# All first keys ahead of the query projection, the projection in three fp32r products, and the input's norm on ScalarE

## The chip, the cores and the metric

The kernel runs on one core of a Trainium2 chip. The metric is the time of one execution on the device in microseconds (us). The engines of the core are TensorE (PE: products and transposes; its weight loads are listed apart as PEld), VectorE (DVE), ScalarE (ACT), GpSimd (POOL) and SyncE (SP, which here only issues loads and stores). They work side by side and wait for each other by semaphores. On each engine the instructions run in the order in which they stand in the program.

## What is computed

A layer of three parts, in fp32, on 8 batches of 64 tokens (512 rows of 512 numbers):

```python
x = x + xattn(layernorm(x), ctx, mask, q_w, q_b, k_w, k_b, v_w, v_b)
x = x + attn(layernorm(x), W_q)
x = x + ffn(layernorm(x), gate_w, gate_b, w1, b1, w2, b2)

def xattn(h, context, mask, ...):          # 16 heads of 32, 1601 context rows per batch
    q = split_heads(h @ q_w.T + q_b)
    k = split_heads(context @ k_w.T + k_b)
    v = split_heads(context @ v_w.T + v_b)
    scores = einsum('bhqd,bhkd->bhqk', q, k) / sqrt(32)
    probs = softmax(where(mask, -inf, scores))
    return join_heads(einsum('bhqk,bhkd->bhqd', probs, v))
```

`attn` is a self-attention without softmax, `ffn` a mixture of 8 experts of which each row takes 2. The change is about the start of `xattn`: the first layernorm, the query projection and the keys of the first batch.

## The kernel before

**Split numbers.** A full fp32 product of 512 columns takes 0.86 us in the profile (the 16 of the query projection take 13.75 us). Most products are made instead from two parts of each operand: the high part is the number rounded to fp32r, the low part the difference to it. `PASSES` lists three products, high by high, high by low, low by high, and `products()` (L847 in its loop) makes them one behind the other for each of the four pieces of 128 rows (C = 4). ACT makes a high part by copying (`copy`, L586, into `kw[0]`, `vw[0]`, `cx[0]`), DVE or POOL the low part by subtracting (`weight_lo` L1287, `ctx_lo` L525, into `cx[1]`). `plain()` (L854) multiplies unsplit fp32 numbers in one product; the query projection uses it, on `qwraw` and the turned input `xnT`.

**Chunks and keys.** The context of a batch arrives in four chunks of 416 columns (`load_chunk`, into the two halves of `raw`). A key item is one of 8 for half of the heads: chunk k = j // 2, row block m = j % 2. PE multiplies into one of four banks (`work`), ACT writes the high part with the bias (`key_hi`, L599), DVE the low part (`key_lo`, L1310), and that frees the bank (`w_free`). In the first batch the loads of chunk 0 and of the first half of the key weights are cut in two by rows (`FIRST_C`, `REST_C`), so that work can start on the first half of the rows. Chunks 0 and 1 get their low parts from DVE, chunks 2 and 3 from POOL.

**The start, on each engine.** SP issues: key weights and chunk 0 in halves, chunk 1, x (`xin`), the query weights (`qwraw`), chunks 2 and 3 (each waits for the low part of the chunk whose half of `raw` it takes), value weights, the other half of the key weights, mask, a second copy of x (`xs`) and the value bias. All go through one hardware queue. PE: keys 0 and 1 (L941, key 0 whole and then key 1), keys 2 and 3, 16 transposes of the normalised input (L950), keys 4 and 5, the query projection (four tiles of 512 tokens into the banks `yb`, that is ptp0 to ptp2 and pv), keys 6 and 7, and then the first batch's body. DVE takes the statistics of `xin` (L1256), and after ACT's root (`root`, L594) a few steps of 4 columns (L1268 to L1272); it then scales the four tiles of `xin` (L1276), which raises `ln1`. ACT copies the transposed tiles to `xnT`, and the projection with the bias to `qT` (L650). DVE builds the blocks `qbd` from `qT` (`query_blocks`, L1324 and L1328), the left operand of the score products (L885). PE may begin them when the blocks, the low parts of all weights (`w_lo`) and an empty bank are there.

**The body** of a batch runs over two halves of the heads. `STEPS` lists its pieces in order: score pairs, value items (two groups of 128 context rows, L847 into `ptp`), exponentials, transposes of the probabilities (L976), weighted sums (L992), and the next keys. POOL's `ctx_lo` for the next batch runs in the second half of each body. POOL also adds the value bias to `xs` (L533, four tiles), which is read after the last batch; this stands between the chunks of batch 0 and those of batch 1.

## Time and profile before

| | us |
|---|---|
| median of 3 runs | 1274.7 |
| lowest and highest of them | 1272.16 and 1274.91 |
| the profiled execution | 1274.62 |
| its span, first to last instruction | 1272.9 |

| part of the program | us from the start of the span |
|---|---|
| PE's first product of keys | 6.4 |
| transposes of the normalised input | 20.5 |
| query projection | 28.7 |
| first score products | 46.9 |
| first value product | 49.1 |

The profile is of one execution. Its page gives busy times per engine and groups of instructions. The timeline lists instructions in order of time, and in brackets how long the engine had been idle before one and what ended that (the releaser). Equal instructions in a row are merged (x4). Matmuls overlap, so the duration of one is longer than the distance from start to start; what a row of them costs is read from the starts. The granted clock of TensorE is a share of 2.4 GHz.

### The profile page before, as it was taken

To read this page: it belongs to the slowest core of one execution; us is meant where nothing else is said; L and a number is where in the kernel's file an instruction comes from. 1 tells how busy PE (TensorE), PEld (TensorE's weight loads), DVE (VectorE), ACT (ScalarE), POOL (GpSimd) and SP (SyncE) were. 2 spreads that over 40 slices of the span, in tenths; PEclk is the share of its full clock that TensorE was granted. 3 is DMA by queue.
4 is the path that set the end of the run, shared out by engine and by line. 5 is a ranking of instruction groups with operands and counts; after the bars stand their busy time and mean duration, and the time that the engine had idled before them with its cause. 6 is when DMAs were issued, how large, how long until landed. Compare 5 with 4: busy or idle time off the path is not lost.

```text
span 1272.9 us, 22193 instructions
## 1 busy us (share of the span) xinstructions
PE 1237.2 (97%) x8493; PEld 1154.6 (91%) x8493; DVE 843.7 (66%) x2197; ACT 674.5 (53%) x1195; POOL 159.3 (13%) x87
## 2 busy tenths in 40 slices
PE   6999999999999999999999999999989999999997
PEld 5799999999999999999999999989768889889896
DVE  4565666566665666656566665686768887877876
ACT  5344544645544553554555446434544767676672
POOL 2203100400310130040022004000022000000011
PEclk9999999999999999999999999999979999999999
DMA  9002200220220031022004002200327677776763
GB/s 333 28 1 88 84 1 1 92 81 1 92 80 1 5 124 44 1 92 80 1 28 144 1 1 92 97 1 1 110 75 259 233 244 263 229 249 235 247 218 103
DMA packets 61683, 129.23 MB, mean 102 GB/s; under 512 B 3660, under 2 KB 21208, under 8 KB 61336
## 3 DMA queue, kind: packets, MB, share of 16 engines
q1 hardware_dynamic: 59416, 121.03, 27.4%
q0 software_dynamic: 2176, 6.95, 1.7%
q8 instruction: 61, 1.00, 0.3%
q14 instruction: 30, 0.25, 0.1%
HBM read 122.07 MB, written 15.34 MB: 108 GB/s over the span
## 4 chain that ended last, share of the span: by engine, by line
PE 91%; DVE 5%; ACT 2%; DMA 1%; issue 1%; POOL 0%; SPq 0%; DVEq 0%; POOLq 0%
PE ptp L847 24%; PE work L847 20%; PE work L1146 8%; PE pv L992 7%; PE ptp L976 7%; PE work L885 6%; PE work L1148 4%; PE ptp L1165 2%; PE ptp L1166 2%; PE ptp L1168 2%; PE ptp L1167 2%; PE ptp L1169 2%; PE work L854 1%; DMA raw<-in_ctxT 1%; DVE pt L1401 1%; ACT pt L586 1%
## 5 line engine op out<-in xcount | busy, mean ns | idle before, releaser
L847 PE MATMUL ptp<-vw_hi,cx_hi 128*128 128x256 f32 x832 | 241.8, 291 | 0.0
L847 PE MATMUL ptp<-vw_hi,cx_lo 128*128 128x256 f32 x832 | 235.4, 283 | 0.0
L847 PE MATMUL ptp<-vw_lo,cx_hi 128*128 128x256 f32 x832 | 235.4, 283 | 0.0
L525 POOL TENSOR_TENSOR cx_lo<-raw,cx_hi 128x1664 fp32r<-128x1664 f32 x30 | 113.8, 3792 | 667.0 <-ACT cx_hi L586 667.0
L847 PE MATMUL work<-cx_hi,kw_hi 128*128 128x400 f32 (+1 forms) x504 | 175.1, 347 | 3.0 <-POOL cx_lo L525 1.7
L847 PEld LDWEIGHTS ptp<-vw_hi,cx_hi 128*128 128x128 f32 x832 | 159.3, 192 | 17.0 <-issue 17.0
L847 PE MATMUL work<-cx_hi,kw_lo 128*128 128x400 f32 (+1 forms) x504 | 173.8, 345 | 0.0
L847 PE MATMUL work<-cx_lo,kw_hi 128*128 128x400 f32 (+1 forms) x504 | 173.4, 344 | 0.0
L1401 DVE TENSOR_TENSOR pt<-ptp,pt 128x512 fp32r<-128x512 f32 (+1 forms) x224 | 141.1, 649 | 34.0 <-ACT pt L586 30.4
L1310 DVE SCALAR_TENSOR_TENSOR kk_lo<-work,biasT,kk_hi 128x400 fp32r<-128x400 f32 (+1 forms) x128 | 78.9, 632 | 122.4 <-ACT kk_hi L599 121.8
L847 PEld LDWEIGHTS ptp<-vw_lo,cx_hi 128*128 128x128 f32 x832 | 159.3, 191 | 0.0
L847 PEld LDWEIGHTS ptp<-vw_hi,cx_lo 128*128 128x128 f32 x832 | 159.3, 191 | 0.0
L1146 PE MATMUL work<-xg,w_hi 128*128 128x384 f32 x512 | 149.2, 361 | 2.7 <-DVE xg L1548 1.3
L586 ACT ACTIVATE pt<-ptp 128x512 fp32r<-128x512 f32 (+1 forms) x224 | 125.0, 567 | 50.4 <-PE ptp L976 47.2
L992 PE MATMUL pv<-pt,vv 128*128 128x256 f32 x806 | 146.2, 303 | 4.3 <-DVE pt L1401 4.3
L599 ACT ACTIVATE kk_hi<-work,biasT 128x400 fp32r<-128x400 f32 (+1 forms) x128 | 74.3, 595 | 131.0 <-PE work L847 128.4
L660 ACT ACTIVATE pr<-pr,nmx 128x1602 f32<-128x1602 f32 x64 | 104.6, 1634 | 70.2 <-DVE nmx L1394 70.2
L1367 DVE TENSOR_TENSOR vv<-ptp,vv 128x256 fp32r<-128x256 f32 (+1 forms) x112 | 45.4, 405 | 144.0 <-ACT vv L586 143.5
L1386 DVE CUSTOM_DVE_ANT_0 pr<-work,negmask 128x400 f32<-128x400 f32 (+1 forms) x256 | 133.7, 569 | 0.5
L613 ACT ACTIVATE vv<-ptp 128x256 fp32r<-128x256 f32 (+1 forms) x112 | 40.7, 364 | 170.7 <-PE ptp L847 170.5
L1148 PE MATMUL work<-xg,w_lo 128*128 128x192 f32 x512 | 128.2, 250 | 0.0
L976 PE MATMUL ptp<-ident,pr 128*128 128x128 f32 x832 | 124.6, 272 | 0.5 <-issue 0.5
(269 smaller groups left out, 2372.0 us busy)
## 6 DMA issues: line engine op xcount, KB each, us to landing
w1raw<-in_w SPq DMA_DIRECT2D x32, 1024.0 KB, 5.1
w2raw<-in_w SPq DMA_DIRECT2D x32, 1024.0 KB, 6.5
raw<-in_ctxT SPq DMA_DIRECT2D x31, 832.0 KB, 6.5
pr<-in_mask SPq DMA_DIRECT2D x8, 800.5 KB, 4.5
xrow<-x_rows SPq DMA_DIRECT2D x7, 256.0 KB, 6.2
y_rows<-y_out_rows POOLq DMA_DIRECT2D x7, 256.0 KB, 2.4
xin<-in_x SPq DMA_DIRECT2D x1, 1024.0 KB, 9.6
qwraw<-in_qwT SPq DMA_DIRECT2D x1, 1024.0 KB, 11.8
```

The source lines that it names most:

```text
L525: pool.tensor_tensor(cx[1][:, :, sl], raw[:, k % 2], cx[0][:, :, sl].bitcast(F32), ALU.subtract).then_inc(c_lo, 1)
L586: act.activation(dst, src, ACT.Copy).then_inc(signal, 1)
L660: act.activation(row, row, ACT.Exp, bias=nmx[:, r:r + 1], accum_out=total).then_inc(exp_done, 1)
L847: last = pe.matmul(dst, lhs(i, c), rhs(j, c), start=(c == 0 and (i, j) == (0, 0)), stop=(c == n - 1 and (i, j) == (1, 0)))
L885: ins = pe.matmul(wide(work[bank_of(last, both[rt])], k), qbd[i][rows, cc, :], kk[j][rows, cc, keys(k)], start=(i, j) == (0, 0), stop=(i, ...
L976: ins = pe.transpose(ptp[j % PTD][:, (2 * n + rt) * P:(2 * n + rt + 1) * P], pr[:, (2 * g + rt) % 4, (first + n) * P:(first + n + 1) * P], ...
L992: ins = pe.matmul(sums[:, rt * 2 * P:(rt + 1) * 2 * P], vv[:, kt, g % 2, rt].rearrange("p a d -> p (a d)"), pt[:, j % PTD, n, rt].rearrang ...
L1146: pe.matmul(work[f][:, 0:2 * SLOTS], w1s[0][:, s, c, f * P:(f + 1) * P], xg[:, c].rearrange("p i n -> p (i n)"), start=c == 0, stop=False)
L1148: last = pe.matmul(work[f][:, 0:SLOTS], w1s[1][:, s, c, f * P:(f + 1) * P], xg[:, c, 0], start=False, stop=c == C - 1)
L1310: dve.scalar_tensor_tensor(out=kk[1][:, m, sl], in0=wide(work[bank], k), scalar=biasT[:, col:col + 1], in1=kk[0][:, m, sl].bitcast(F32), o ...
L1386: dve.tensor_tensor_reduce(pr[:, a % 4, sl], wide(bank, k), negmask[:, sl], SCALE, LOWEST, ALU.add, ALU.max, smx[:, a, k:k + 1]).then_inc( ...
L1401: dve.tensor_tensor(pt[:, j % PTD, 0:n, :, 1, :], ptp[j % PTD][:, 0:n * 2 * P].rearrange("p (n r d) -> p n r d", n=n, r=2), pt[:, j % PTD, ...
```

## The change

It does the following.

- PE: keys 0 and 1 are made side by side, half of the rows at a time in each of the three products. Keys 6 and 7 come ahead of the query projection, and the projection is made by `products()` from split operands, 48 products in place of 16.
- ACT writes the high parts `xnT[0]` and `qw_hi`, DVE the low parts `xnT[1]` and `qw_lo`.
- ACT applies the norm: DVE makes the bias, minus mean times scale, in one small step (`ln_scale`), and ACT scales the four tiles of `xin` with it. Its copy of chunk 2 moves ahead of the root, its copy of chunk 3 ahead of key 3.
- SP issues the query weights behind chunks 2 and 3. `kwraw` now holds one half of the columns, so the load of the second half waits until the low parts of the first are made.
- DVE's work on the value weights, the query blocks, the second half of the key weights and the mask moves behind its low parts of keys 6 and 7.
- POOL's four sums on `xs` move behind its chunks of batch 4.

ACT, from the high part of key 0 on: before, the root, the copy of chunk 2, two keys, the turned input, then keys 4 and 5 around chunk 3 (`cx_hi<-raw` is a chunk).

```order
L594 ACTIVATE stat<-stat 128x4 [waits variance_ready]
L586 ACTIVATE cx_hi<-raw 128x4x416 [waits context_chunk_loaded0]
L599 ACTIVATE kk_hi<-work,biasT 128x400 [waits work_bank_full] x2
L586 ACTIVATE xnT<-ptp 128x512 [waits pre_psum_full] x3
L586 ACTIVATE xnT<-pv 128x512 [waits pre_psum_full]
L599 ACTIVATE kk_hi<-work,biasT 128x400 [waits work_bank_full]
L586 ACTIVATE cx_hi<-raw 128x4x416 [waits context_chunk_loaded1]
L599 ACTIVATE kk_hi<-work,biasT 128x400 [waits work_bank_full]
L586 ACTIVATE vw_hi<-pr 128x2048 [waits v_weight_loaded]
```

The same place of ACT now:

```order
L597 ACTIVATE cx_hi<-raw 128x4x416 [waits context_chunk_loaded0]
L605 ACTIVATE stat<-stat 128x4 [waits variance_ready]
L652 ACTIVATE xin<-xin,stat 128x512 [waits x_scale_ready]
L652 ACTIVATE xin<-xin,stat 128x512 x3
L610 ACTIVATE kk_hi<-work,biasT 128x400 [waits work_bank_full]
L597 ACTIVATE cx_hi<-raw 128x4x416 [waits context_chunk_loaded1]
L610 ACTIVATE kk_hi<-work,biasT 128x400 [waits work_bank_full]
L597 ACTIVATE xnT_hi<-ptp 128x512 [waits pre_psum_full] x3
L597 ACTIVATE xnT_hi<-pv 128x512 [waits pre_psum_full]
L597 ACTIVATE qw_hi<-qwraw 128x2048 [waits q_weight_loaded]
L610 ACTIVATE kk_hi<-work,biasT 128x400 [waits work_bank_full] x2
L610 ACTIVATE kk_hi<-work,biasT 128x402 [waits work_bank_full] x2
```

The root now stands behind chunk 2, four scalings are new, and the query weights' high part stands ahead of keys 4 to 7.

DVE, from the scaling of the input to the first step of the body, before:

```order
L1276 TENSOR_SCALAR xin<-xin,stat 128x512 [waits vector_step]
L1276 TENSOR_SCALAR xin<-xin,stat 128x512 x3
L1310 SCALAR_TENSOR_TENSOR kk_lo<-work,biasT,kk_hi 128x400 [waits keys_values_hi] x6
L1287 TENSOR_TENSOR vw_lo<-pr,vw_hi 128x2048 [waits weight_hi]
L1324 CAST qbd_hi<-qT 32x2x64 [waits queries_ready,constants_ready]
...
L1287 TENSOR_TENSOR kw_lo<-kwraw,kw_hi 128x4x256 [waits weight_hi]
L1282 TENSOR_SCALAR negmask<-pr 128x1601 [waits mask_loaded]
L1310 SCALAR_TENSOR_TENSOR kk_lo<-work,biasT,kk_hi 128x402 [waits keys_values_hi] x2
```

The same place of DVE now:

```order
L1328 SCALAR_TENSOR_TENSOR stat<-stat 128x4 [waits vector_step]
L1335 SCALAR_TENSOR_TENSOR kk_lo<-work,biasT,kk_hi 128x400 [waits keys_values_hi] x4
L1478 TENSOR_TENSOR xnT_lo<-ptp,xnT_hi 128x512 [waits pre_psum_drained] x3
L1478 TENSOR_TENSOR xnT_lo<-pv,xnT_hi 128x512 [waits pre_psum_drained]
L1335 SCALAR_TENSOR_TENSOR kk_lo<-work,biasT,kk_hi 128x400 [waits keys_values_hi] x2
L1481 TENSOR_TENSOR qw_lo<-qwraw,qw_hi 128x2048 [waits q_weight_hi]
L1335 SCALAR_TENSOR_TENSOR kk_lo<-work,biasT,kk_hi 128x402 [waits keys_values_hi] x2
L1310 TENSOR_TENSOR vw_lo<-pr,vw_hi 128x2048 [waits weight_hi]
L1349 CAST qbd_hi<-qT 32x2x64 [waits queries_ready,constants_ready]
```

The low part of the query weights stands between the keys' low parts, and nothing of the keys is left behind the query blocks.

The diff, cut to its core:

```diff
-            xin = sb(m, "xin", [P, TT, D], F32)
-            xnT = sb(m, "xnT", [P, C, T], F32)
-            qwraw = sb(m, "qwraw", [P, C, D], F32)
-            kwraw = sb(m, "kwraw", [P, C, D], F32)
+            with ExitStack() as m2:
+                xin = sb(m2, "xin", [P, TT, D], F32)
+            qw_hi = sb(m, "qw_hi", [P, C, D], F32R)
+            xnT = [sb(m, f"xnT_{n}", [P, C, T], F32R) for n in ("hi", "lo")]
+            with ExitStack() as m2:
+                qwraw = sb(m2, "qwraw", [P, C, D], F32)
+            qw_lo = sb(m, "qw_lo", [P, C, D], F32R)
+            kwraw = sb(m, "kwraw", [P, C, D // 2], F32)
...
+        qw = [qw_hi, qw_lo]
...
+        ln_scale = sem("x_scale_ready")
...
+        q_hi, q_lo = sem("q_weight_hi"), sem("q_weight_lo")
+        xt_lo = sem("x_turned_lo")
...
-                sp.dma_start(kwraw[:, :, cols], kwT[:, cols].rearrange("(c p) n -> p c n", p=P)).then_inc(ld_kw[h], 16)
+                sp.wait_ge(kw0_lo, 1)
+                sp.wait_ge(w_lo, 1)
+                sp.dma_start(kwraw[:], kwT[:, cols].rearrange("(c p) n -> p c n", p=P)).then_inc(ld_kw[h], 16)
...
-                sp.dma_start(kwraw[:, cs, 0:D // 2], kwT[rows, 0:D // 2].rearrange("(c p) n -> p c n", p=P)
+                sp.dma_start(kwraw[:, cs], kwT[rows, 0:D // 2].rearrange("(c p) n -> p c n", p=P)
...
-            sp.dma_start(qwraw[:], qwT.rearrange("(c p) n -> p c n", p=P)).then_inc(ld_qw, 16)
...
+            sp.dma_start(qwraw[:], qwT.rearrange("(c p) n -> p c n", p=P)).then_inc(ld_qw, 16)
...
                 ctx_lo(0, k)
-            pool.wait_ge(ld2[0], 32)
-            for t in range(TT):
-                pool.tensor_tensor(xs[:, t], xs[:, t], vb, ALU.add).then_inc(vb_done, 1)
             for b in range(1, B):
...
                     ctx_lo(b, k)
+                if b == B // 2:
+                    pool.wait_ge(ld2[0], 32)
+                    for t in range(TT):
+                        pool.tensor_tensor(xs[:, t], xs[:, t], vb, ALU.add).then_inc(vb_done, 1)
             pool.wait_ge(c_lo, NKC * B)
...
             act.wait_ge(ld_kw0, 16)
-            copy(kw[0][:, FIRST_C, first], kwraw[:, FIRST_C, first], kw0_hi)
+            copy(kw[0][:, FIRST_C, first], kwraw[:, FIRST_C], kw0_hi)
             act.wait_ge(ld_c0, 16)
...
             act.wait_ge(ld_kw[0], 16)
-            copy(kw[0][:, REST_C, first], kwraw[:, REST_C, first], w_hi)
+            copy(kw[0][:, REST_C, first], kwraw[:, REST_C], w_hi)
             act.wait_ge(ld_raw[0], 16)
...
             first_keys(range(0, 2))
+            ctx_hi(0, 2)
             root(1, range(TT))
-            ctx_hi(0, 2)
-            first_keys(range(2, 4))
+            act.wait_ge(ln_scale, 1)
+            for t in range(TT):
+                act.activation(xin[:, t], xin[:, t], ACT.Identity, bias=stat[:, 52 + t:53 + t],
+                               scale=stat[:, 32 + t:33 + t]).then_inc(ln1, 1)
+            first_keys(range(2, 3))
+            ctx_hi(0, 3)
+            first_keys(range(3, 4))
             for c in range(C):
                 act.wait_ge(t_full, c + 2)
-                copy(xnT[:, c], yb[c][:], t_out)
-            first_keys(range(4, 5))
-            ctx_hi(0, 3)
-            first_keys(range(5, 6))
+                copy(xnT[0][:, c], yb[c][:], t_out)
+            act.wait_ge(ld_qw, 16)
+            copy(qw_hi[:], qwraw[:], q_hi)
+            first_keys(range(4, FIRST_K))
             act.wait_ge(ld_vw, 32)
...
                     act.wait_ge(ld_kw[1], 16)
-                    copy(kw[0][:, :, D // 2:D], kwraw[:, :, D // 2:D], w_hi)
-            first_keys(range(6, FIRST_K))
+                    copy(kw[0][:, :, D // 2:D], kwraw[:], w_hi)
...
             READY = {(0, 0): ((kw0_hi, w_hi), (c0_hi, c_hi)), (0, 1): ((c0_lo, c_lo),), (1, 0): ((kw0_lo, w_lo),)}
-            for m in range(2):
-                for i, j in PASSES:
-                    for c in range(C):
-                        if m == 0 and c % (C // 2) == 0:
-                            for ready in READY[i, j]:
-                                pe.wait_ge(ready[c // (C // 2)], 1)
-                        last = pe.matmul(work[m][:, 0:KC], kw[i][:, c, m * P:(m + 1) * P], cx[j][:, c, 0:KC],
-                                         start=(c == 0 and (i, j) == PASSES[0]), stop=(c == C - 1 and (i, j) == PASSES[-1]))
-                last.then_inc(w_full, 1)
+            for i, j in PASSES:
+                for half, cs in enumerate((FIRST_C, REST_C)):
+                    for ready in READY[i, j]:
+                        pe.wait_ge(ready[half], 1)
+                    for m in range(2):
+                        for c in range(cs.start, cs.stop):
+                            first, final = c == 0 and (i, j) == PASSES[0], c == C - 1 and (i, j) == PASSES[-1]
+                            last = pe.matmul(work[m][:, 0:KC], kw[i][:, c, m * P:(m + 1) * P], cx[j][:, c, 0:KC],
+                                             start=first, stop=final)
+                            if final:
+                                last.then_inc(w_full, 1)
             for j in range(2, 4):
...
                 last.then_inc(t_full, 1)
-            for j in range(4, 6):
+            for j in range(4, FIRST_K):
                 pe.wait_ge(w_free, j - 3)
                 key_item(0, 0, j, work[j % 4])
-            pe.wait_ge(t_out, C + 1)
-            pe.wait_ge(ld_qw, 16)
+            pe.wait_ge(xt_lo, C)
+            pe.wait_ge(q_lo, 1)
             for m_ in range(C):
-                plain(yb[m_][:], lambda c: qwraw[:, c, m_ * P:(m_ + 1) * P],
-                      lambda c: xnT[:, c]).then_inc(t_full, 1)
-            for j in range(6, FIRST_K):
-                pe.wait_ge(w_free, j - 3)
-                key_item(0, 0, j, work[j % 4])
+                products(yb[m_][:], lambda i, c: qw[i][:, c, m_ * P:(m_ + 1) * P],
+                         lambda i, c: xnT[i][:, c]).then_inc(t_full, 1)
             pe.wait_ge(w_lo, 3)
...
-            def layer_norm(src, dst, signal, o, ts=range(TT)):
+            def norm_weights(o, ts):
...
+
+            def normed(src, dst, signal, t):
+
+                dve.tensor_scalar(dst[:, t], src[:, t], mv[:, t, 0:1], stat[:, 32 + t:33 + t],
+                                  ALU.subtract, ALU.mult).then_inc(signal, 1)
+
+            def layer_norm(src, dst, signal, o, ts=range(TT)):
+
+                norm_weights(o, ts)
                 for t in ts:
-                    dve.tensor_scalar(dst[:, t], src[:, t], mv[:, t, 0:1], stat[:, 32 + t:33 + t],
-                                      ALU.subtract, ALU.mult).then_inc(signal, 1)
+                    normed(src, dst, signal, t)
...
                 dve.wait_ge(kw_ready, 1)
-                dve.tensor_tensor(kw[1][:, cs, first], kwraw[:, cs, first], kw[0][:, cs, first].bitcast(F32),
+                dve.tensor_tensor(kw[1][:, cs, first], kwraw[:, cs], kw[0][:, cs, first].bitcast(F32),
                                   ALU.subtract).then_inc(kw_done, 1)
...
-            layer_norm(xin, xin, ln1, 1)
+            norm_weights(1, range(TT))
+            dve.scalar_tensor_tensor(out=stat[:, 52:52 + TT], in0=mv[:, :, 0], scalar=-1.0, in1=stat[:, 32:32 + TT],
+                                     op0=ALU.mult, op1=ALU.mult).then_inc(ln_scale, 1)
...
+                if j == 4:
+                    for c in range(C):
+                        dve.wait_ge(t_out, c + 2)
+                        dve.tensor_tensor(xnT[1][:, c], yb[c][:], xnT[0][:, c].bitcast(F32), ALU.subtract).then_inc(xt_lo, 1)
...
-                    weight_lo(2, [w[:].rearrange("p (a b) n -> p a b n", a=2) for w in vw], vwraw)
-                    dve.wait_ge(consts, 5)
-                    dve.wait_ge(q_done, 2)
-                    query_blocks(0, 0)
-                    weight_lo(3, [w[:, :, D // 2:D] for w in kw], kwraw[:, :, D // 2:D])
-                    convert_mask(0)
+                    dve.wait_ge(q_hi, 1)
+                    dve.tensor_tensor(qw_lo[:], qwraw[:], qw_hi[:].bitcast(F32), ALU.subtract).then_inc(q_lo, 1)
...
+            weight_lo(2, [w[:].rearrange("p (a b) n -> p a b n", a=2) for w in vw], vwraw)
+            dve.wait_ge(consts, 5)
+            dve.wait_ge(q_done, 2)
+            query_blocks(0, 0)
+            weight_lo(3, [w[:, :, D // 2:D] for w in kw], kwraw[:])
+            convert_mask(0)
...
```

## Rows read from the trace of the kernel before

**Rows 1.** The page: busy time of each engine; a group of instructions, busy, mean ns.

```profile
PE 1237.2 (97%) x8493; PEld 1154.6 (91%) x8493; DVE 843.7 (66%) x2197; ACT 674.5 (53%) x1195; POOL 159.3 (13%) x87
...
L599 ACT ACTIVATE kk_hi<-work,biasT 128x400 fp32r<-128x400 f32 (+1 forms) x128 | 74.3, 595 | 131.0 <-PE work L847 128.4
```

**Rows 2.** Waits of PE, 50 to 770 us: total us, times, longest.

```profile
PE pv L992 <- DVE pt L1401: 2.3, 13, 0.2
```

**Rows 3.** Timeline of PE to 50 us: start us, us, instruction, idle before it.

```profile
11.71 1.53 PE L941 MATMUL work<-cx_hi,kw_lo 128*128 128x400 f32 x4
13.04 0.93 PE L941 MATMUL work<-cx_hi,kw_hi 128*128 128x400 f32 x4
...
20.54 1.53 PE L950 MATMUL ptp<-ident,xin 128*128 128x128 f32 x12 [0.80 <-DVE xin L1276]
...
24.22 0.42 PE L847 MATMUL work<-cx_hi,kw_hi 128*128 128x400 f32 x1 [1.72 <-POOL cx_lo L525]
...
28.70 10.46 PE L854 MATMUL ptp<-xnT,qwraw 128*128 128x512 f32 x24
...
46.93 0.45 PE L885 MATMUL work<-kk_hi,qbd_hi 64*128 64x400 f32 x2
...
48.36 0.45 PE L885 MATMUL work<-kk_hi,qbd_hi 64*128 64x400 f32 x2 [0.61 <-DVE kk_lo L1310]
...
49.10 0.39 PE L847 MATMUL ptp<-vw_hi,cx_hi 128*128 128x256 f32 x1
```

**Rows 4.** The chain that ended last, 10 to 19 us: start us, us, what.

```profile
10.51 7.93 DMA raw<-in_ctxT
```

**Rows 5.** Timeline of ACT, 17 to 30 us.

```profile
17.32 0.20 ACT L594 ACTIVATE stat<-stat 128x4 f32<-128x4 f32 x1 [1.28 <-DVE stat L1266]
18.46 1.60 ACT L586 ACTIVATE cx_hi<-raw 128x1664 fp32r<-128x1664 f32 x1 [0.94 <-DMA raw<-in_ctxT]
...
21.23 1.57 ACT L586 ACTIVATE xnT<-ptp 128x512 f32<-128x512 f32 x3 [0.21 <-PE ptp L950]
...
29.39 1.90 ACT L586 ACTIVATE vw_hi<-pr 128x2048 fp32r<-128x2048 f32 x1
```

**Rows 6.** Timeline of POOL, 20 to 40 us.

```profile
20.23 3.84 POOL L525 TENSOR_TENSOR cx_lo<-raw,cx_hi 128x1664 fp32r<-128x1664 f32 x1 [17.79 <-ACT cx_hi L586]
...
32.55 6.99 POOL L533 TENSOR_TENSOR xs<-xs,hn 128x512 f32<-128x512 f32 x4
```

**Rows 7.** Timeline of SP, the issues of x and the query weights.

```profile
3.84 0.51 SPq L417 DMA_DIRECT2D xin<-in_x  x1
4.39 1.02 SPq L418 DMA_DIRECT2D qwraw<-in_qwT  x1
```

**Rows 8.** The page, DMA issues: KB each, us from issue to landing.

```profile
xin<-in_x SPq DMA_DIRECT2D x1, 1024.0 KB, 9.6
qwraw<-in_qwT SPq DMA_DIRECT2D x1, 1024.0 KB, 11.8
```

**Rows 9.** Timeline of DVE, 18 to 75 us.

```profile
18.37 0.16 DVE L1272 TENSOR_TENSOR stat<-stat 128x4 f32<-128x4 f32 x1
...
31.32 3.42 DVE L1287 TENSOR_TENSOR vw_lo<-pr,vw_hi 128x2048 fp32r<-128x2048 f32 x1 [1.16 <-ACT vw_hi L586]
36.56 3.31 DVE L1324 CAST qbd_hi<-qT 32x128 fp32r<-32x128 f32 x4 [1.82 <-ACT qT L650]
...
41.17 1.23 DVE L1287 TENSOR_TENSOR kw_lo<-kwraw,kw_hi 128x1024 fp32r<-128x1024 f32 x1
...
73.74 0.96 DVE L1324 CAST qbd_hi<-qT 32x128 fp32r<-32x128 f32 x4
```

**Rows 10.** Timeline of PE in the expert stage, first and last of 15 products.

```profile
999.76 0.39 PE L1165 MATMUL ptp<-w_hi,h 128*128 128x512 f32 x1
...
1002.96 0.39 PE L1169 MATMUL ptp<-w_lo,h 128*128 128x512 f32 x1
```

**Rows 11.** Busy time by stretches: PE, PEld, DVE, ACT, POOL, granted clock, DMA, GB/s.

```profile
950.00:955.00 5.00, 5.00 (x25) 5.00 (x25) 3.30 (x7) 0.49 (x1) 4.12 (x3) 0.50 0.14 52
```

## The prediction

> **What bounds the kernel now.** I read first the busy times of the engines, then who TensorE (PE) waits for from 50 to 770 us, then its timeline up to 50 us, and last the other engines' timelines beside it. PE is busy for 97% of the span [rows 1], and in the attention from 50 to 770 us it waits 2.3 us in all, in 13 waits of at most 0.2 us [rows 2]. So in the attention a microsecond saved before its first value product is a microsecond off the end, as long as nothing new holds PE. The change works almost only before that product, which starts at 49.10 us [rows 3]. That start is the mark that I count towards.
>
> From 20 us to the mark the reader should see four pieces in PE's rows [rows 3]. The transposes start at 20.54, when x is normalised, and end 1.96 us later, at 22.50. Then 1.72 us are lost until GpSimd (POOL) has the low part of chunk 2. Keys 4 and 5 take 24.22 to 28.70, so 2.24 us each. The query projection runs from 28.70 for 13.75 us (keys 6 and 7 need 4.48 us and end at 46.93). Last come two pairs of score products: the first starts at 46.93, the second at 48.36, since it needs the bank that VectorE (DVE) empties after the last key; a pair alone takes 0.74 us (48.36 to 49.10), so 0.69 us are lost. POOL is late because chunk 2 is: its load, issued at 10.51, lands 7.93 us later, at 18.4 [rows 4], ScalarE (ACT) copies it in 1.60 us [rows 5], POOL subtracts in 3.84 us from 20.23 [rows 6].
>
> **The change part by part.**
>
> Loads. The query weights go behind chunks 2 and 3. The x load is issued at 3.84 and takes 9.6 us, the query weights at 4.39 [rows 7] and take 11.8 [rows 8]: they land at 13.4 and 16.2, so the weights occupy the queue for 2.75 us, and chunk 2 follows them. Without them it lands at 18.4 - 2.75, about 15.7. The query weights then follow chunk 3: roughly 21, needed on ACT at 25.3 (below). The second half of the key weights gets a wait that is over by then (the low parts of its predecessor are what keys 0 and 1 multiply), so it holds nothing.
>
> First two keys. The products of the first rows, four instead of two, run while the rest is still loading. Before 13.04 four products take 1.33 us, after it 0.76 [rows 3]: 0.33 against 0.19 us each, which for 400 columns is TensorE's level of 1.2 GHz and then that of 2.4. Two of the later, fast products are saved: keys 0 and 1 end at 14.9 instead of 15.24, keys 2 and 3 (4.48 us) at 19.35. Key 0 is complete later than before, which only ACT notices: it has both high parts by 15.7.
>
> Normalised x. ACT now copies chunk 2 at 15.7 to 17.3, ahead of the root, which started at 17.32 before [rows 5]: no loss. DVE's small steps end at 18.53 as before [rows 9], one more of their size gives 18.75. Then ACT scales four tiles of 512 columns in place of DVE. A single one of 400 columns takes 0.6 us [rows 1], three copies of 512 took 1.57 us together [rows 5], so they start some 0.48 us apart: 2.05 us for four, to 20.8. If scaled ones don't overlap, it is 4 times 0.6, to 21.2. I take 20.8, 0.3 us later than before, since nothing stands between the four; the other end is 21.2. In the gap from 19.35 PE idles 1.45 us.
>
> Chunk 2 on POOL: 17.4 to 21.3, ahead of the end of the transposes at 22.8. The wait of 1.72 us is gone. Keys 4 to 7 follow without a break: 4 times 2.24, to 31.75. Chunk 3 on ACT is queued behind the scaling and key 2's high part (0.5 us): 21.3 to 22.9, then 3.8 us on POOL to 26.8; key 6 wants it at 27.3. That cover is 0.5 us thin.
>
> Query projection. 16 full fp32 products went in 13.75 us, 0.86 each. Now there are 48 fp32r products of 512 columns. The same shape in the expert stage: 14 starts from 999.76 to 1002.96, so 0.229 us apart [rows 10], and 48 of them are 11.0 us. Saved: 2.8 us. By the Trainium skill (TensorE: Matmul & The Clock Gate, Back-to-back issue gap) a warm product of 512 columns costs N/2.4 + 2.5 ns, an estimate of 0.216 us, and the 48 would be 10.4 us; the rows of this kernel read 0.229, and the sum goes by them.
>
> What the projection now waits for. ACT: chunk 3's copy ends at 22.9, key 3's high part (0.5 us when it follows another instruction), four turned tiles (2.05 us), to about 25.3; the query weights' high part, 2048 columns as in vw_hi, 1.90 us [rows 5], to 27.2; keys 4 and 5 to 28.2. DVE then takes their low parts to 28.8 and the low part of the query weights. Its cost is not in the trace: 1024 columns took 1.23 us [rows 9], so 2.4 us, while 2048 columns in vw_lo took 3.42, with POOL's sums, which began at 32.55 [rows 6], beside it. With POOL idle after 26.8 I take 2.4: ready at 31.2, 0.5 us ahead of PE. At 3.4 it is 32.2, and PE stands for 0.5. The Trainium skill (GPSIMD Engine Reference, Key points) says that POOL shares its SBUF interfaces with DVE and gets in the way of DVE instructions with two SBUF inputs. The trace agrees (3.42 against 2 times 1.23), and by it the sums, had they stayed, would have cost that 0.5 us; that is their whole worth here.
>
> From 31.75 the projection ends at 42.7. The first scores need the query blocks and the low part of the other half of the key weights. ACT: value weights to 34.3, query tile 1 at 37.9. DVE: vw_lo to 37.7 at the latest, query blocks 0.96 us [rows 9] and 1.2 us more, to 40.1, key weights to 41.3. With POOL beside it the first part took 3.31 us [rows 9]; then it would be 43.7 and PE would stand for 1.0. POOL is idle now, so I take nothing. The banks of the scores have long been empty, so the 0.69 us of loss go too. Two pairs: 1.48 us, and the first value product starts at 44.2.
>
> POOL's sums, 7.0 us from 32.55 before [rows 6], lie in the middle of the attention, after the subtractions for batch 4. POOL is busy for 13% of the span [rows 1]. They could lengthen a DVE instruction by 1 us, and PE's margins there are not seen in the rows; I put 0, upper end 1.0.
>
> **Sum.** 1.72 (wait for POOL) - 0.3 (transposes later) + 2.8 (projection) + 0.7 (scores) = 4.9 us, the same as 49.10 - 44.2. The profiled execution took 1274.62 us (span 1272.9), next to the median of 1274.7. So 1274.6 - 4.9 = 1269.7.
>
> **Rivals.**
> - Chunk 2 is not early. If it lands at 18.4 as before, ACT copies it to 20.0, and root, scaling and transposes hang behind it: x is ready at 23.5 in place of 20.8. Gain 2.2 us: 1272.4. Against it: the rows on the loads look like one queue in order. For it: ACT now has the root behind that copy, which before it had not.
> - The thin covers tear (chunk 3 on POOL, low query weights, query blocks): 0.5 to 1.5 us less, 1270.2 to 1271.2; I put it at 1270.9.
> - Slower: the clock. PE idles 1.45 us from 19.35 in one piece, directly before the keys. If TensorE goes to 1.2 GHz there and stays until the projection, 48 key products cost 0.14 us more each, 6.9 us: 1276.6. It decides from 34 such products on. Against it: before, idle times of 0.80 and 1.72 us were followed by products at full speed [rows 3]. That the clock follows how busy the array was is also what the Trainium skill says (TensorE: Matmul & The Clock Gate, What's actually happening).
> - The late low clock falls otherwise. From 950 to 955 us, in the router stage, the granted clock is 0.50 with PE busy throughout [rows 11]. If a shifted execution is spared that, it wins another 2.5 us: 1267.2. The runs of before, 1272.16 to 1274.91, are 2.75 us apart, as if one had been spared it; this is luck, not the change.
> - It does nothing: the end is set elsewhere. Only possible if the expert stage waited for loads that don't move; they are released by the work itself, so hardly.
>
> **How the numbers follow.** Forecast 0.50, torn covers 0.16, chunk 2 not early 0.15, late clock spared 0.10, slower 0.06, nothing 0.03. A measurement of this kernel can tell about 0.2%, 2.5 us, from no change, so the border is at 1272.2. Faster: 0.50 + 0.16 + 0.10 and a small part of the third, 0.80. Same: the rest of the third and the last, 0.14. Slower: 0.06. Range: down to the spared clock, 1267.4, up past chunk 2 being late, 1272.8.
>
> **What would show it.** Right: chunk 2's load lands before 16 us; the transposes start near 20.8 and keys 4 to 7 follow without idle time; 48 products of 512 columns 0.229 us apart from 31.8; no idle time between projection and scores; first value product at 44.2. Wrong: a wait of PE for the low query weights, for POOL at key 6 or for the query blocks; x ready after 22; key products 0.33 us apart after 20 us.

## The result and the profile after

The changed kernel takes 1274.86 us (median of 19 runs, 1272.95 to 1277.28). The kernel before, run beside it, takes 1273.11 (19 runs, 1271.46 to 1275.86). The ratio is 1.0013, 95% interval 1.0007 to 1.0019: 1.7 us longer, between 0.9 and 2.4, where the forecast was 4.9 us shorter. The difference is below what I had called measurable, but the interval excludes a gain. The profiled execution took 1273.95 us, its span is 1272.1.

The waits of PE from 0 to 60 us in the changed kernel (total us, times, longest), and behind them the one wait from 50 to 770 us:

```profile
PE ptp L968 <- ACT xin L652: 5.7, 1, 5.7
PE work L958 <- ACT cx_hi L597: 4.4, 2, 3.6
...
PE pv L1007 <- DVE pt L1426: 2.3, 13, 0.2
```

The attention is as tight as before [rows 2]. The new loss is one wait of 5.7 us for ACT's scaling of x. PE's timeline shows what lies around it:

```profile
25.65 2.82 PE L968 MATMUL ptp<-ident,xin 128*128 128x128 f32 x12 [5.71 <-ACT xin L652]
28.27 0.84 PE L968 MATMUL pv<-ident,xin 128*128 128x128 f32 x4
28.86 0.43 PE L863 MATMUL work<-cx_hi,kw_hi 128*128 128x400 f32 x1
...
37.77 0.39 PE L863 MATMUL ptp<-xnT_hi,qw_hi 128*128 128x512 f32 x1
...
48.76 0.45 PE L901 MATMUL work<-kk_hi,qbd_hi 64*128 64x400 f32 x2
...
50.05 0.38 PE L863 MATMUL ptp<-vw_hi,cx_hi 128*128 128x256 f32 x1
```

The transposes start at 25.65; I had put them at 20.8. They last 3.21 us until key 4, where they lasted 1.96 [rows 3]. Behind them all goes as forecast: four keys without a break in 8.91 us, the projection in 10.99 until the scores, no idle time between, 1.29 us for two score pairs. The mark is 50.05 in place of 49.10 [rows 3].

Why ACT is late stands on DVE's timeline (start us, us, instruction, in brackets the idle time before it):

```profile
16.44 0.17 DVE L1281 TENSOR_SCALAR stat<-stat 128x4 f32<-128x4 f32 x1
18.05 0.18 DVE L1283 RECIPROCAL stat<-stat 128x4 f32<-128x4 f32 x1 [1.44 <-ACT stat L605]
18.26 3.59 DVE L1284 TENSOR_TENSOR stat<-stat 128x4 f32<-128x4 f32 x1
21.88 0.16 DVE L1285 TENSOR_TENSOR stat<-stat 128x4 f32<-128x4 f32 x1
...
22.48 0.16 DVE L1328 SCALAR_TENSOR_TENSOR stat<-stat 128x4 f32<-128x4 f32 x1
```

A multiplication of 4 columns takes 3.59 us; its like take 0.16. Beside it, on POOL and on ACT:

```profile
18.10 3.73 POOL L535 TENSOR_TENSOR cx_lo<-raw,cx_hi 128x1664 fp32r<-128x1664 f32 x1 [15.65 <-ACT cx_hi L597]
```

```profile
16.33 1.60 ACT L597 ACTIVATE cx_hi<-raw 128x1664 fp32r<-128x1664 f32 x1
17.81 0.20 ACT L605 ACTIVATE stat<-stat 128x4 f32<-128x4 f32 x1
22.67 2.92 ACT L652 ACTIVATE xin<-xin,stat 128x512 f32<-128x512 f32 x4 [4.66 <-DVE stat L1328]
```

POOL's subtraction for chunk 2 runs from 18.10 to 21.83, and DVE's small step from 18.26 to 21.85: both end together. The Trainium skill (GPSIMD Engine Reference, Key points) says that POOL shares its SBUF interfaces with DVE, at the cost of DVE instructions in a 2-port perf mode or with two SBUF inputs. This row, with two inputs, agrees, and gives the size: the step was held for as long as POOL's instruction ran. The order in ACT's rows makes the meeting: chunk 2 was copied ahead of the root, so POOL started just as DVE's steps did.

### The profile page after: what moved, and what is told of

Same layout as the page of the kernel before. It is cut to its first block, busy times and chain, and to the rows that moved or that the text cites. A ratio compares the mean times of both kernels' runs of the same rounds, so it can differ in the third digit from the quotient of the medians.

```text
span 1272.1 us, 22233 instructions
## 1 busy us (share of the span) xinstructions
PE 1235.9 (97%) x8509; PEld 1159.2 (91%) x8509; DVE 847.1 (67%) x2199; ACT 679.3 (53%) x1200; POOL 156.2 (12%) x87
## 4 chain that ended last, share of the span: by engine, by line
PE 91%; DVE 5%; ACT 2%; issue 1%; DMA 0%; SPq 0%; DVEq 0%; ACTq 0%
PE ptp L863 25%; PE work L863 20%; PE work L1161 8%; PE pv L1007 7%; PE ptp L991 7%; PE work L901 6%; PE work L1163 3%; PE ptp L1180 2%; PE ptp L1181 2%; PE ptp L1183 2%; PE ptp L1182 2%; PE ptp L1184 2%; PE work L870 1%; DVE pt L1426 1%; ACT pt L597 1%
```

## Experiments

**Theory A.** A DVE instruction on SBUF that is issued while POOL's long subtraction runs is held until that ends. So x is late, PE idles for 5.7 us, and the clock falls for the transposes. **Rival B.** The root itself, or ACT's new scaling, makes x late whatever POOL does. **Rival C.** The order in general is worse, and POOL's overlap is a coincidence.

In what follows the mark is the start of the first value product. It is counted from the start of the span, and the first loads land up to some 1 us earlier or later from one execution to the next: ACT's root, which needs the statistics of x, starts at 17.32 in the kernel before [rows 5] and between 16.55 and 16.85 in the seven executions below in which it has no chunk ahead of it and the loads go as in the changed kernel. So marks of two executions are compared to about 0.7 us, and times by their intervals. All ratios are to the kernel before.

### The root ahead of chunk 2

```diff
-            ctx_hi(0, 2)
             root(1, range(TT))
+            ctx_hi(0, 2)
             act.wait_ge(ln_scale, 1)
```

> The changed kernel with one line moved: ScalarE takes the root ahead of its copy of chunk 2, so GpSimd's subtraction of chunk 2 starts behind VectorE's small steps and not inside them. Theory A (VectorE's step on 4 columns with two SBUF inputs stands still for as long as GpSimd's long subtraction runs, 3.59 us): the step L1284 takes under 0.3 us, the steps end near 18.1, GpSimd starts near 18.5, the four scalings end near 21.3, the transposes take 2.0 us and not 3.2 since the array no longer idles 5.7 us, and the first value product starts at 44.6 in place of 50.05. Time 5.4 us below the changed kernel, some 1269.5, ratio to the kernel before 0.997. Theory B (the step is long for a reason of its own, such as the loads in flight or the wait behind the root): the step still takes over 3 us, and the first value product stays at 49 to 50.

Measured: 1269.68 us (6 runs), ratio 0.9972 (0.9960 to 0.9984), mark 44.06. The rows of DVE, of POOL and of PE in this kernel:

```profile
17.05 0.16 DVE L1284 TENSOR_TENSOR stat<-stat 128x4 f32<-128x4 f32 x1
```

```profile
18.47 3.73 POOL L535 TENSOR_TENSOR cx_lo<-raw,cx_hi 128x1664 fp32r<-128x1664 f32 x1 [16.01 <-ACT cx_hi L597]
```

```profile
21.16 1.53 PE L968 MATMUL ptp<-ident,xin 128*128 128x128 f32 x12 [2.37 <-ACT xin L652]
```

The same step takes 0.16 us, since POOL starts 0.5 us after the last small step ends. One line brings the forecast time about. This version beats both kernels: by 3.6 us (2.0 to 5.1) the one before, and by some 5 us the changed one.

### The same order, but POOL waits for the small steps

```diff
             pool.wait_ge(c_lo, 2)
+            pool.wait_ge(ln_scale, 1)
             for k in range(2, NKC):
```

> The changed kernel with one wait more: GpSimd starts its subtraction of chunk 2 only when the scale of the input's norm is ready; ScalarE's order is that of the changed kernel. Theory A: the step L1284 takes under 0.3 us although root and copy stand as in the changed kernel; scale ready near 19.2, scalings end at 22.1, GpSimd works from 19.3 to 23.1, first value product at 45.4 us. Time some 4.6 us below the changed kernel. Theory B: the step still takes over 3 us, GpSimd starts only near 22.7 and ends at 26.5, and the first value product is at 50 or later.

Measured: 1270.65 us (10 runs), ratio 0.9978 (0.9969 to 0.9987), mark 45.65. ACT's order is that of the changed kernel, and still the step is short. DVE, then POOL:

```profile
18.77 0.17 DVE L1285 TENSOR_TENSOR stat<-stat 128x4 f32<-128x4 f32 x1
```

```profile
19.97 3.72 POOL L535 TENSOR_TENSOR cx_lo<-raw,cx_hi 128x1664 fp32r<-128x1664 f32 x1 [17.53 <-DVE stat L1329]
```

Only POOL's start was moved, and the mark falls by 4.4 us, from 50.05: rivals B and C fall with it. The root behind chunk 2 costs little by itself. From the end of the statistics to the transposes there are 5.46 us here (17.29 to 22.75) and 4.60 in the version above (16.56 to 21.16), so 0.9 us.

### The subtraction in four pieces

```diff
-            for k in range(2, NKC):
-                ctx_lo(0, k)
+            pool.wait_ge(c_hi, 3)
+            for c in range(C):
+                ins = pool.tensor_tensor(cx[1][:, c, 2 * CC:3 * CC], raw[:, 0, c], cx[0][:, c, 2 * CC:3 * CC].bitcast(F32),
+                                         ALU.subtract)
+            ins.then_inc(c_lo, 1)
+            ctx_lo(0, 3)
```

> The changed kernel with GpSimd's subtraction of chunk 2 in four instructions of 416 columns in place of one of 1664. Theory A, if VectorE is let in only between two GpSimd instructions: no step is longer than about 1.1 us, but several of the steps with two inputs are lengthened, and the steps together end 1 to 4 us late as before; first value product between 47 and 50. Theory A2 (both share the bandwidth while GpSimd works, without a lock): the step L1284 alone still takes about 3.6 us or ends in the middle of a piece. Theory B: L1284 3.6 us, independent of the pieces.

Measured: 1276.8 us (one run), mark 49.47. DVE, and POOL beside it:

```profile
17.05 0.80 DVE L1288 TENSOR_TENSOR stat<-stat 128x4 f32<-128x4 f32 x1
17.89 1.00 DVE L1289 TENSOR_TENSOR stat<-stat 128x4 f32<-128x4 f32 x1
18.92 0.99 DVE L1290 TENSOR_SCALAR stat<-stat 128x4 f32<-128x4 f32 x1
19.94 0.98 DVE L1291 TENSOR_TENSOR stat<-stat 128x4 f32<-128x4 f32 x1
20.96 0.16 DVE L1332 SCALAR_TENSOR_TENSOR stat<-stat 128x4 f32<-128x4 f32 x1
```

```profile
16.75 4.15 POOL L541 TENSOR_TENSOR cx_lo<-raw,cx_hi 128x416 fp32r<-128x416 f32 x4 [14.30 <-ACT cx_hi L601]
```

Four pieces take 4.15 us, 1.04 each. Each of four small steps is held for one piece, and the fifth, after the last piece, is not. So one DVE instruction gets in between two of POOL's, and the hold is as long as what is left of POOL's current instruction. Shorter pieces don't help a chain of small steps, for it loses one piece per step. L1290 has a single tensor as input, and is held as well; whether the skill's words on the perf mode cover it, no row shows. The reciprocal just ahead of these steps (16.83, also with one input) took its usual 0.18 us although POOL's row starts at 16.75. Whether such a step is let through, or POOL was not yet at work, no run tells.

### The kernel before, with chunk 2 early and ahead of the root

```diff
-            sp.dma_start(qwraw[:], qwT.rearrange("(c p) n -> p c n", p=P)).then_inc(ld_qw, 16)
             load_chunk(0, 2)
             load_chunk(0, 3)
+            sp.dma_start(qwraw[:], qwT.rearrange("(c p) n -> p c n", p=P)).then_inc(ld_qw, 16)
...
-            root(1, range(TT))
             ctx_hi(0, 2)
+            root(1, range(TT))
```

> The kernel before with two moves only: the load of the query weights goes behind chunks 2 and 3, and ScalarE copies chunk 2 ahead of the root. VectorE still scales the input and the projection is plain fp32. Theory A: GpSimd starts near 18 inside VectorE's small steps, the second of them (L1269) is held for 3 us or more, x is normalised near 24.3, the transposes run at half clock, and the first value product starts at 52.5 in place of 49.10; the time is 3 us above the kernel before (ratio 1.002 to 1.003). Theory B (the loss comes from what is new in the changed kernel: scaling on ScalarE, new operands): no step over 1 us, first value product at 47 to 49, time equal or 1 to 2 us less.

Measured: 1277.08 us (9 runs), ratio 1.0034 (1.0023 to 1.0044), mark 54.04. DVE, then PE:

```profile
18.82 3.57 DVE L1269 TENSOR_TENSOR stat<-stat 128x4 f32<-128x4 f32 x1
```

```profile
24.99 2.82 PE L950 MATMUL ptp<-ident,xin 128*128 128x128 f32 x12 [5.25 <-DVE xin L1276]
```

Two moves out of the change, made in the old kernel, bring the loss. The mark is 1.5 us later than the expected 52.5, in which transposes at half the clock were already counted. The transposes start at 24.99 in place of 24.3, which is 0.7 us. The other 0.8 lie behind them: the first key products ran at half the clock as well (0.33 us apart until 30.1), so keys 4 and 5 took 5.32 us, from 28.31 to 33.63, in place of 4.48.

### The kernel before, with the load alone moved

The same edit to the loads as above, and nothing else: ACT keeps the root ahead of chunk 2.

> The kernel before with one edit: the query weights' load goes behind chunks 2 and 3; ACT keeps the root ahead of chunk 2. Chunk 2 then lands near 15.7 us, ACT copies it right behind the root (17.5 to 19.1), POOL subtracts from 19.1 to 22.9. If a long GpSimd subtraction holds DVE instructions on SBUF operands that are issued while it runs: DVE's scaling of x, issued from 18.5, loses a tile to it, ends near 23.5 in place of 20.5, and the first value product starts at 50.4 to 51.6 in place of 49.10; 1274.4 to 1275.6 us, although the wait of 1.72 us for POOL is gone. If the scaling is not held: transposes at 20.5 as before, no wait for POOL, first value product near 47.4, 1271.3 us.

Measured: 1275.67 us (10 runs), ratio 1.0023 (1.0011 to 1.0034), mark 49.97. DVE, then POOL:

```profile
17.98 5.32 DVE L1276 TENSOR_SCALAR xin<-xin,stat 128x512 f32<-128x512 f32 x4
```

```profile
18.60 3.96 POOL L525 TENSOR_TENSOR cx_lo<-raw,cx_hi 128x1664 fp32r<-128x1664 f32 x1 [16.15 <-ACT cx_hi L586]
```

The four scalings took 5.32 us. One of them took 3.94, the others 0.53 to 0.54 each. PE's wait of 1.72 us for POOL is gone, and a wait of 3.08 us for x has come. In the kernel before, the late chunk kept POOL out of DVE's way: POOL started at 20.23 [rows 6], as the scalings ended. The gain that I had booked for the early chunk is negative as long as DVE scales x. The mark is 0.4 us ahead of the expected 50.4 to 51.6, and 0.9 us behind the one before, where the time is 2.9 us longer (1.4 to 4.3); the sign agrees, the two sizes don't quite.

### DVE scales x in the changed kernel

The version with the root ahead, with ACT's four scalings taken out and DVE's put back in their place:

```diff
-            act.wait_ge(ln_scale, 1)
-            for t in range(TT):
-                act.activation(xin[:, t], xin[:, t], ACT.Identity, bias=stat[:, 52 + t:53 + t],
-                               scale=stat[:, 32 + t:33 + t]).then_inc(ln1, 1)
...
+            for t in range(TT):
+                normed(xin, xin, ln1, t)
```

> Kernel e1_root_first with VectorE scaling the input as in the kernel before (one SBUF input, 0.48 us apart), so that the scaling by ScalarE is undone alone. GpSimd starts on chunk 2 near 18.5, when one or two of the four tiles are scaled. Theory A as the pieces showed it (also a step with a single SBUF input, L1290, was held for 0.99 us): the next tile is held until GpSimd is through at 22.2, the transposes start near 23.2 to 24.2, in place of 21.16, at half clock, and the first value product at 47 to 48. If only instructions with two SBUF inputs are held: the tiles are done at 19.9, the transposes are early, and the first value product starts near 43.3, bound by GpSimd's end at 22.2.

Measured: 1275.32 us (10 runs), ratio 1.0014 (1.0004 to 1.0023), mark 51.44. DVE, POOL, and PE:

```profile
17.80 8.68 DVE L1289 TENSOR_SCALAR xin<-xin,stat 128x512 f32<-128x512 f32 x4
```

```profile
18.43 7.78 POOL L535 TENSOR_TENSOR cx_lo<-raw,cx_hi 128x1664 fp32r<-128x1664 f32 x2 [15.98 <-ACT cx_hi L597]
```

```profile
26.54 2.82 PE L964 MATMUL ptp<-ident,xin 128*128 128x128 f32 x12 [7.31 <-DVE xin L1289]
```

The mark came 3.4 us behind the expected 47 to 48: that allows for one hold, and there were two. Without the scalings ACT has chunk 3 ready in time as well, POOL runs two subtractions back to back, and two of DVE's tiles are held for one each (longest 3.94 us, shortest 0.54). So moving the scaling to ACT is worth 5.3 us by the two ratios (0.9972 against 1.0014) once chunk 2 is early, though ACT is slower at it. The early chunk needs the other edit: while DVE scales x it loses, here and in the experiment above. The reverse doesn't hold. The scaling on ACT with the late chunk (the load of the query weights back, below) loses nothing that the times show.

### Plain projection

The version with the root ahead, with the 16 plain fp32 products of before:

```diff
-                products(yb[m_][:], lambda i, c: qw[i][:, c, m_ * P:(m_ + 1) * P],
-                         lambda i, c: xnT[i][:, c]).then_inc(t_full, 1)
+                plain(yb[m_][:], lambda c: qwraw[:, c, m_ * P:(m_ + 1) * P],
+                      lambda c: xnT[:, c]).then_inc(t_full, 1)
```

> Kernel e1_root_first (the changed kernel with the root ahead of the copy of chunk 2) with the projection as it was: 16 fp32 products, no split of the query weights and of the turned input. In e1 the first value product starts at 44.06 us. If the projection term of the sum was right (13.75 us against 11.0), that start moves by 2.8 us to 46.8, and the time rises to 1272.3. If the split projection cost more than its products (weight loads, ScalarE and VectorE busy with the parts), the difference is under 2 us.

Measured: 1272.43 us (10 runs), ratio 0.9991 (0.9982 to 1.0001), mark 46.99. The mark is 2.93 us later than with three fp32r products; I had booked 2.8. This term was right.

### The sums back

POOL's four sums on `xs` stand again between the chunks of batches 0 and 1:

```diff
+            pool.wait_ge(ld2[0], 32)
+            for t in range(TT):
+                pool.tensor_tensor(xs[:, t], xs[:, t], vb, ALU.add).then_inc(vb_done, 1)
             for b in range(1, B):
...
-                if b == B // 2:
-                    pool.wait_ge(ld2[0], 32)
-                    for t in range(TT):
-                        pool.tensor_tensor(xs[:, t], xs[:, t], vb, ALU.add).then_inc(vb_done, 1)
```

> Kernel e1_root_first with GpSimd's four sums back behind the chunks of batch 0. Theory A (an instruction of VectorE and one of GpSimd that both need the shared access to SBUF go one after the other): the sums start when their load has landed, near 29 to 30 us, and lie beside the low parts of the query weights (2.28 us in e1) or of the value weights and the query blocks; one or more of these take 1 to 3 us longer, and GpSimd's first sum too. The low query weights were ready 0.8 us ahead of TensorE in e1, so the first value product moves by 0 to 2 us from 44.06. If nothing of VectorE is longer than in e1, theory A is too broad.

Measured: 1269.07 us (one run), first scores at 42.89, where the version without this edit has 42.77. The sums' place is worth nothing here. I had said 0.5 us. They start at 30.72, since they wait for the value bias. DVE's subtraction for the low query weights (28.99, 2.28 us) is under way by then and is not lengthened; the sum is, 1.71 us where the next two take 1.29. What the sums do hold are the low value weights, 2.58 us in place of 2.29, and PE doesn't wait for these. The fourth sum, issued beside them, took 3.33:

```profile
34.51 2.58 DVE L1309 TENSOR_TENSOR vw_lo<-pr,vw_hi 128x2048 fp32r<-128x2048 f32 x1 [1.17 <-ACT vw_hi L596]
34.90 3.33 POOL L543 TENSOR_TENSOR xs<-xs,hn 128x512 f32<-128x512 f32 x1
```

So the hold works both ways: of two such subtractions or sums, the one that is issued second waits for the other. This also puts right a reading in the prediction. In the kernel before, DVE's 3.42 us for the low value weights, from 31.32 [rows 9], were not the sums' doing. POOL's rows of that kernel:

```profile
28.86 3.73 POOL L525 TENSOR_TENSOR cx_lo<-raw,cx_hi 128x1664 fp32r<-128x1664 f32 x1 [4.78 <-ACT cx_hi L586]
32.55 3.31 POOL L533 TENSOR_TENSOR xs<-xs,hn 128x512 f32<-128x512 f32 x1
```

The subtraction for chunk 3 ran until 32.59 and held DVE's, which ended 2.15 us later, about what it takes alone. The first sum waited for it: 3.31 us, where the other three took 1.27.

### Scaling into another tile

```diff
-                act.activation(xin[:, t], xin[:, t], ACT.Identity, bias=stat[:, 52 + t:53 + t],
+                act.activation(qT[:, t], xin[:, t], ACT.Identity, bias=stat[:, 52 + t:53 + t],
...
-                    last = pe.transpose(yb[c][:, t * P:(t + 1) * P], xin[:, t, c * P:(c + 1) * P], ident[:])
+                    last = pe.transpose(yb[c][:, t * P:(t + 1) * P], qT[:, t, c * P:(c + 1) * P], ident[:])
```

> Kernel e1_root_first with ScalarE writing the scaled input to the query tile, which is free then, and the transposes reading it there. In e1 the four scalings take 2.91 us, 0.73 each, against the 0.48 that I had put from copies out of PSUM. If that is because each writes over its own input, they now take about 2.1 us and the first value product starts at 43.3. If it is the scale and bias per partition, or the reading from SBUF, it stays at 2.9 and 44.06.

Measured: 1268.38 us (one run). ACT in this kernel, and in the changed kernel the four copies of the same size out of PSUM (three and one):

```profile
18.21 2.91 ACT L652 ACTIVATE qT<-xin,stat 128x512 f32<-128x512 f32 x4
```

```profile
27.94 1.55 ACT L597 ACTIVATE xnT_hi<-ptp 128x512 fp32r<-128x512 f32 x3
29.38 0.61 ACT L597 ACTIVATE xnT_hi<-pv 128x512 fp32r<-128x512 f32 x1
```

Four scalings take 2.91 us whether in place or not. Each lasts 0.80 us and they start 0.71 apart; the copies last 0.60 and start 0.48 apart. That a scaling writes where it reads is not the cause. The source in SBUF is hardly it either: ACT's copy of 512 columns of the key weights, out of SBUF, lasts 0.63 us in both kernels. What is left is the scale and the bias from a tensor: with a bias alone (`qT<-ptp,biasT`, 512 columns out of PSUM) an instruction lasts 0.69. No run changed only these.

### The load of the query weights back

The version with the root ahead, with the query weights' load ahead of chunks 2 and 3 again.

> The version with the root ahead of chunk 2, with the query weights' load back in its old place ahead of chunks 2 and 3. If the moved load is what brings chunk 2 early: its load lands near 18.4 us in place of under 16, ACT copies it from 18.5 to 20.1 and scales only then, so the four scalings end near 23.0, the transposes start near 23.0 in place of 21.16, and the first value product starts near 45.8 to 47.1 in place of 44.06 (the upper end if the transposes fall to half the clock after 3.3 us of idle time): 1271.5 to 1272.8 us. If chunk 2 comes early for another reason (or the order of the loads does not matter), nothing moves: first value product 44.1, 1269.7 us.

Measured: 1270.22 us (10 runs), ratio 0.9976 (0.9965 to 0.9988), mark 45.26. The chain of waits (start us, us, what) names the load, and PE's row the effect:

```profile
9.96 7.90 DMA raw<-in_ctxT
17.86 0.02 issue
17.88 1.60 ACT cx_hi L597
19.48 2.83 ACT xin L652 x4
```

```profile
22.35 1.53 PE L968 MATMUL ptp<-ident,xin 128*128 128x128 f32 x12 [2.86 <-ACT xin L652]
```

Chunk 2 lands at 17.9, as before the change (18.4 [rows 4]), and the transposes start 1.2 us later than with the load moved. The early chunk is worth about 1.2 us at the mark, in this order of ACT's; the times, 0.5 us apart, are within their intervals of each other, so the time doesn't show it. The mark is 0.5 us ahead of the expected range, since the chunk landed 0.5 ahead of the 18.4 that it was worked out from.

### Keys 0 and 1 one behind the other

The version with the root ahead, with the first two keys as in the kernel before.

> The version with the root ahead of chunk 2, with keys 0 and 1 made one behind the other again, as in the kernel before. What this order is worth while TensorE waits for x anyway: keys 2 and 3 end some 0.4 to 1.0 us later, at about 19.5 in place of 18.7, which shortens the idle time ahead of the transposes (2.37 us) and moves nothing behind it; transposes near 21.2, first value product near 44.1, 1269.7 us. If the order matters by what ACT gets earlier or later (the high parts of keys 0 and 1 ahead of the root and chunk 2), the transposes move by the same time that the root does, up to 0.5 us either way.

Measured: 1269.17 us (10 runs), ratio 0.9971 (0.9961 to 0.9980), mark 44.32. PE's idle time ahead of the transposes is 1.78 us in place of 2.37, the start 21.41, 0.25 later, as is the root (16.85 and 16.59). The difference in idle time is not the order's: two executions above with keys by halves and the root ahead (plain projection, sums back) idle 1.43 and 1.45 us. The order by halves is worth nothing that these runs show while PE waits for x.

### The gap filled

The changed kernel, with 30 more products in the gap ahead of the transposes. Nothing uses them.

```diff
+            for n_ in range(30):
+                pe.matmul(yb[0][:, 0:KC], kw[0][:, n_ % C, 0:P], cx[0][:, n_ % C, 0:KC], start=True, stop=True)
             pe.wait_ge(ln1, TT)
```

> The changed kernel with 30 more products of 400 columns (into a bank that the transposes overwrite) in the gap in which TensorE idles for 5.7 us ahead of the transposes; their result is used by nothing. They take 30 times 0.183, some 5.5 us. If the granted clock of 0.50 in the transposes comes from the idle time before them: the transposes start at 25.6 as before, the clock stays at 1.00, they take 2.0 us in place of 3.2, and the first value product starts near 48.8 in place of 50.05; about 1273.6 us where the changed kernel has 1274.9, although PE makes 30 products more. If the low clock there has another cause, the transposes take 3.2 us again, the first value product stays at 50.05 or later, 1274.9 us.

Measured: 1273.15 us (10 runs), ratio 0.9998 (0.9986 to 1.0010), mark 47.35. Busy time by stretches of the changed kernel (stretch, length, PE, PEld, DVE, ACT, POOL, granted clock, DMA, GB/s):

```profile
19.70:25.60 5.90, 0.25 (x2) 0.00 (x0) 3.89 (x7) 2.93 (x5) 2.13 (x1) 0.69 1.06 408
25.60:26.60 1.00, 0.95 (x5) 0.95 (x6) 0.49 (x1) 1.00 (x2) 0.00 (x0) 0.50 0.93 369
...
28.80:31.00 2.20, 2.20 (x15) 2.20 (x14) 2.20 (x4) 2.20 (x4) 2.20 (x1) 1.00 1.05 381
```

The same of the kernel with the gap filled, and PE's row there:

```profile
24.40:26.20 1.80, 1.76 (x17) 1.76 (x17) 0.63 (x1) 1.80 (x2) 0.00 (x0) 1.00 0.97 394
```

```profile
24.44 1.53 PE L970 MATMUL ptp<-ident,xin 128*128 128x128 f32 x12 [0.90 <-ACT xin L652]
```

With an idle gap the clock is 0.50, that is 1.2 GHz, and the transposes last 3.21 us until key 4; with 30 useless products ahead it is 1.00 and they last 1.73 (24.44 to 26.17). The low clock came from the idle time and cost 1.5 us. DVE's step was held here too (3.63 us). The mark is 2.7 us earlier, of which 1.26 is an earlier start (the held step begins at 17.00 in place of 18.26) and 1.44 the clock. The Trainium skill (TensorE: Matmul & The Clock Gate, What's actually happening) says that the clock follows how busy the array is; the two rows agree.

## Why the prediction was wrong, point by point

1. *What bounds the kernel.* Right. Every version moved its time in the direction of its mark (plain projection and the gap filled within their intervals), and the attention stayed tight.
2. *Loads.* Right: chunk 2 was early. Its copy started at 16.33, behind the high parts of keys 0 and 1, without a wait for the load. Where ACT did wait for it, the copy started at 15.06 (the gap filled) and at 16.88 (the old kernel with chunk 2 ahead), around the 15.7 forecast. That this gains the 1.72 us wait is wrong by itself: in the kernel before the moved load alone gives 1.0023.
3. *First two keys.* Forecast to end at 14.9, ended at 15.46, and ACT did wait for them. Both high parts came back to back (15.36, 1.08 us for the two) where one had been done at 13.34 before, and only then did ACT copy chunk 2, at 16.33 in place of 15.7. The root behind it started at 17.81 in place of 17.3. PE itself got nothing from the order.
4. *Normalised x: the step that failed.* "ACT now copies chunk 2 at 15.7 to 17.3, ahead of the root, which started at 17.32 before [rows 5]: no loss. DVE's small steps end at 18.53 as before [rows 9], one more of their size gives 18.75." I took durations from rows in which POOL was idle (POOL started at 20.23 [rows 6], the steps had ended at 18.53 [rows 9]), and the next paragraph put POOL's chunk 2 at 17.4 to 21.3, right over them. I cited the rule on POOL and DVE for the low query weights, where it made 0.5 us, and didn't lay it over the steps that I had just moved under POOL. The steps ended at 22.64 in place of 18.75: 3.4 us by the hold, 0.5 by the root at 17.81.
5. *Four scalings.* Forecast 2.05 us, bound 2.4, measured 2.92: 0.9 too little. The 0.48 us from start to start came from copies, without scale or bias, and the bound of 0.6 us for one from 400 columns with a bias. Measured were 0.80 for one and 0.71 from start to start. The trace of the kernel before had a nearer row that I didn't use, 512 columns with a bias: 0.69 (`qT`).
6. *Transposes.* 1.25 us too little. The clock was a rival in my list, at an idle time of 1.45 us; with 5.7 us it came true, for the 16 transposes, while the key products behind them ran at full speed.
7. *Sum of the miss.* 3.4 (hold) + 0.5 (root) + 0.9 (scalings) + 1.25 (clock) - 0.2 (scores) = 5.85 us, that is 50.05 - 44.2; the first three terms make x late, the fourth is the longer transposes, the last the score pairs, which took 1.29 us in place of 1.48. With the root ahead of chunk 2, hold and clock go and the mark is 44.06, near the forecast for reasons that partly cancel: scalings 0.9 slower, root 0.7 earlier.
8. *Projection.* Right: 48 products in 10.99 us, forecast 11.0 from a distance of 0.229 us [rows 10].
9. *Thin covers* (chunk 3 on POOL, low query weights, query blocks). None tore: PE waited for none of them. With the root ahead of chunk 2, where PE is as early as forecast, the low query weights are ready at 31.17 (DVE's row: 28.89 and 2.28 us) and PE comes to them some 0.6 us later; I had put 0.5. The dearer price of 3.4 us for them rested on a wrong reading: the 3.42 us of the low value weights lay under POOL's subtraction for chunk 3 and not under the sums.
10. *Scores.* Right: no idle time between projection and scores.
11. *Sums on POOL.* Right at 0 in their new place, wrong on their old one (0.5 us booked, 0 measured), by the same wrong reading.
12. *The slower rival* had the right sign and the wrong cause. The rival that should have been there is one sentence: POOL now overlaps the small steps.

The rival on the late stretch of low clock in the router stage came true in part, and by luck. From 952 to 956 us, the kernel before and then the changed one:

```profile
952.00:956.00 4.00, 3.86 (x21) 3.68 (x20) 1.30 (x7) 0.59 (x2) 3.18 (x3) 0.60 0.34 131
952.00:956.00 4.00, 3.38 (x23) 3.20 (x21) 1.75 (x8) 0.98 (x2) 3.40 (x3) 0.78 0.31 119
```

From the mark to the end of the span there are 1223.8 us in the profiled execution before and 1222.05 after, with nothing changed there that PE waits for. An estimate of what the low clock costs there is the length of each stretch of 5 us times what its granted clock lacks of 1.00: 6.85 us before, 5.15 after. All fourteen profiled executions fall into three groups: 5.1 to 5.2 us lost and 1221.3 to 1222.4 from mark to end (seven), 6.8 to 6.9 and 1223.1 to 1223.8 (four), 8.5 to 8.6 and 1224.7 to 1225.6 (three). So this stretch explains most of what single executions differ by behind the mark, up to 4 us; what puts an execution into one group or another stays open. It is also why the two profiled ones stand in the wrong order (1274.62 and 1273.95). Only the medians of many runs show the loss.

## What to carry to other kernels

Before an instruction is moved earlier on one engine, write down which instructions of the *other* engines it then lies over, and read their durations from rows with the same neighbour. In these runs a long POOL subtraction on SBUF held the DVE steps, scalings and subtractions with all tensors in SBUF that were issued under it, until it ended, and DVE's subtractions held POOL's sums. So a chain of tiny steps on which much depends must be over before POOL starts: put POOL's trigger behind it, by the order on the engine that releases POOL or by a wait. And an edit may be worth something only beside another: the early chunk lost as long as DVE scaled x.
